# Gathered rows added on TensorE instead of VectorE, in pairs of one kind, with wider compare slots

## The chip, the cores and the metric

One core of one Trainium2 chip. The metric is the device time of one execution in microseconds, the median of three runs.

## The reference

A graph layer over 12,500 nodes with 64 features and 400,000 edges. The edges are sorted by `dst`, and `dst` is drawn so that low nodes have many edges.

```
msg = x[src] + edge_attr
agg = segment_sum(msg, dst, num_segments=12500)
h   = relu(agg @ W1 + b1)
y   = h @ W2 + b2
out = layernorm(x + y)      # over the 64 features, no scale or shift
```

All inputs are float32, `src` and `dst` int32. W1 is 64 x 128, W2 is 128 x 64.

## The kernel before

The sum over edges is done by one-hot products on TensorE, and it has two parts.

**The edge part.** The edges are cut into 625 chunks of 640. A chunk lies in SBUF as 128 partitions x 5 tiles x 64 features. VectorE makes its one-hot (`mark`, L835: node position in a window of 64 nodes, or of 32, against the edge's own), TensorE multiplies the five tiles of rows with the five tiles of the one-hot into `chunk_ps` (`products`, L1059), and VectorE adds the result to `lists`, the sums by node (`add`, L856). Two chunks make a pair: they go to the two halves of the TensorE columns and of the PSUM bank. All of this is float32, and each float32 matmul stands in the trace as two records, so a pair is 10 matmuls and 20 records.

**The x part, in two ways.** The last 205 chunks are *gathered*: GpSimd (POOL) fetches `x[src]` with one indirect DMA for each tile (L572, five a chunk, 1,025 in all) into `xmsg`, and VectorE adds that to the edge rows in `gmsg` (`mix`, L828) before TensorE takes them. The first 420 chunks (`CROWS` = 84 rows of five) are *counted*: nothing is gathered for them. Instead the kernel counts how often each source node occurs for each destination and multiplies these counts by x. A *pass* compares 128 edges of one window of 1 to 4 nodes: VectorE makes two bf16 one-hots for several passes at once (a *slot*, `make_slot`: `oh_lo` L874 and `oh_key` L878, at most 10 passes or 980 key columns), TensorE multiplies them pass by pass into `counted_ps` (L1076), ScalarE copies each finished unit of up to five nodes to `counts` (L674). 128 rows of counts are a *block*; a block is multiplied by x in 98 matmuls of 193 columns (L1092, x split in three bf16 parts), spread by `MULTIPLY` over the slots that follow, and turned (L1104) and added to `lists` (L865). The edges of 128 passes are a *group*: VectorE searches where they begin (L788), POOL fetches their records (L581), TensorE turns them into a table (`turn_table`, L1033).

**What sets the order.** Each engine has one program, written out before the launch. `plan` chooses window width and nodes of each unit by a cost per pass, and fills the slots. `timeline` gives each slot a planned begin, by a cost per slot, between 90 us and `LAST`, and hangs gathers (`GATHERS_AT`) and chunks (`JOBS_AT`) before the slot whose planned begin is due. Nothing waits for a planned time; the engines wait for semaphores only. POOL may gather as far ahead as `xmsg` has buffers (`XSLOTS` = 5 chunks) and waits for `mixed` of the chunk that held the buffer. SP loads the edge rows (`gmsg`, `GSLOTS` = 8, and `cmsg`, `CSLOTS` = 6) as `summed` frees them.

**Before and behind the main loop.** POOL first writes the list of all passes with iotas on one partition (L541, a run of equal windows at a time, once for the node and once for the run). Then it starts to gather; SP sends the list on and loads what the searches need. Behind the loop come the last block, a test whether any count was out of range, and the two-layer network with the norm over node blocks.

## Time and profile before

| | us |
|---|---|
| median of three runs (1505.83 to 1508.44) | 1507.69 |
| the profiled execution | 1504.08 |
| its span, from the first to the last instruction | 1502.3 |
| PE busy, of the span | 1212.9 |
| VectorE (DVE) busy | 1346.7 |
| ScalarE (ACT) busy | 840.6 |
| GpSimd (POOL) busy | 1076.9 |
| mean granted TensorE clock, of 1 | 0.921 |

PE is the matmul side of TensorE and PEld its weight loads, which overlap. Times in the views count from the first instruction of the profiled execution. Instructions of one engine overlap by some tens of ns, so what one costs in a row of many is read from start to start. The slices of the page show three parts: to 86 us preparation, to 1415 us the main loop, and from there the end.

### The profile page before, as it was taken

Reading aid. Unit: us, or ns where it says so; the run is one execution under the profiler, and the core shown is the slowest. Engines: PE = TensorE matmul, PEld = TensorE weight load, DVE = VectorE, ACT = ScalarE, POOL = GpSimd, SP = SyncE. Lnnn points to the kernel's source line nnn. Section 1 sums busy time; section 2 is a strip of 40 time slices with the busy share of each in tenths; the row PEclk is TensorE's granted clock in tenths of the full one; section 3 lists DMA queues with packets and bytes.
Section 4 is the critical chain, followed back from the end, with each engine's and each line's share of the span. In section 5 each row is a group of like instructions: output and inputs, shape, how many; then the busy total and the mean of one; then the engine's idle time right before and its main releaser. Section 6 shows DMA issues by size and latency. Waiting matters only on the chain.

```text
span 1502.3 us, 43214 instructions
## 1 busy us (share of the span) xinstructions
PE 1212.9 (81%) x15541; PEld 979.2 (65%) x15542; DVE 1346.7 (90%) x3537; ACT 840.6 (56%) x1767; POOL 1076.9 (72%) x1139
## 2 busy tenths in 40 slices
PE   1235767778787887888888888899999999999895
PEld 1134656655666776776655555688888888888853
DVE  4659999999999899899999999999999999999644
ACT  1044444668435566567444444567777777766454
POOL 9758777777777777777777777777777777777312
PEclk8555578999999999999999999999999999999997
DMA  2833444444444444444444443444444444433133
GB/s 103 212 85 79 120 113 111 116 111 109 108 115 112 114 115 106 108 109 116 112 114 107 104 117 102 113 112 111 112 112 109 111 113 113 113 100 94 23 79 93
DMA packets 159272, 162.50 MB, mean 108 GB/s; under 512 B 53817, under 2 KB 141801, under 8 KB 158729
## 3 DMA queue, kind: packets, MB, share of 16 engines
q1 hardware_dynamic: 124679, 122.86, 27.9%
q0 software_dynamic: 34384, 36.90, 12.8%
q8 instruction: 126, 2.06, 0.6%
q14 instruction: 83, 0.68, 0.1%
HBM read 154.78 MB, written 4.85 MB: 106 GB/s over the span
## 4 chain that ended last, share of the span: by engine, by line
PE 31%; DVE 29%; issue 16%; POOL 11%; DVEq 4%; ACT 2%; DMA 1%; POOLq 0%; ACTq 0%
PE sums_ps L1092 12%; PE counted_ps L1076 11%; POOL xmsg L572 11%; DVE oh_key L878 10%; DVE oh_lo L874 6%; PE chunk_ps L1059 5%; DVE onehot L835 5%; DVE lists L856 3%; DVE gmsg L828 2%; DVEq L848 2%; PE turn_ps L1104 2%; ACT counts L674 1%; DVE less_b L788 1%; DVEq L856 1%; PE counted_ps L1160 1%
## 5 line engine op out<-in xcount | busy, mean ns | idle before, releaser
L572 POOL DMA_INDIRECT xmsg<-in_x,idx_t x1025 | 995.5, 971 | 322.4 <-issue 307.8
L674 ACT CAST counts<-counted_ps 128x392 bf16<-128x392 f32 (+2 forms) x1375 | 675.2, 545 | 480.6 <-PE counted_ps L1076 468.1
L1076 PE MATMUL counted_ps<-oh_key,oh_lo 128*128 128x196 bf16 (+3 forms) x4206 | 524.7, 255 | 123.2 <-DVE oh_key L878 105.9
L878 DVE TENSOR_TENSOR oh_key<-counted_ps,tables 128x980 bf16<-128x980 f16 (+4 forms) x883 | 541.3, 613 | 0.0
L1092 PE MATMUL sums_ps<-x_parts,counts 128*128 128x193 bf16 (+4 forms) x4410 | 495.0, 249 | 0.3
L1076 PEld LDWEIGHTS counted_ps<-oh_key,oh_lo 128*128 128x128 bf16 x4206 | 290.5, 102 | 227.3 <-DVE oh_key L878 167.0
L1092 PEld LDWEIGHTS sums_ps<-x_parts,counts 128*128 128x128 bf16 (+4 forms) x4410 | 396.3, 109 | 38.6 <-issue 1.9
L874 DVE TENSOR_TENSOR oh_lo<-counted_ps,tables 128x640 bf16<-128x640 f16 (+3 forms) x883 | 412.3, 467 | 9.9 <-PE counted_ps L1076 1.0
L1059 PE MATMUL chunk_ps<-onehot,cmsg 128*64 128x32 f32 (+1 forms) x4200 | 254.1, 231 | 26.2 <-DVE gmsg L828 23.6
L1059 PEld LDWEIGHTS chunk_ps<-onehot,cmsg 128*64 128x64 f32 x4200 | 220.1, 145 | 60.9 <-issue 43.2
L835 DVE TENSOR_TENSOR onehot<-counted_ps,rel_t 128x160 f32<-128x160 f32 (+1 forms) x625 | 234.3, 375 | 0.2
L1059 PE MATMUL chunk_ps<-onehot,gmsg 128*64 128x64 f32 x2050 | 172.8, 238 | 19.8 <-DVE onehot L835 16.7
L1059 PEld LDWEIGHTS chunk_ps<-onehot,gmsg 128*64 128x64 f32 x2050 | 145.1, 148 | 37.4 <-DVE lists L856 26.1
L856 DVE TENSOR_TENSOR lists<-lists,chunk_ps 64x32 f32 (+1 forms) x625 | 121.8, 195 | 43.4 <-PE chunk_ps L1059 17.6
L828 DVE TENSOR_TENSOR gmsg<-gmsg,xmsg 128x320 f32<-128x320 f32 x205 | 97.8, 477 | 2.2 <-DMA xmsg<-in_x,idx_t 2.1
L613 POOL TENSOR_TENSOR x_parts<-x_parts,rstd 128x512 f32<-128x512 f32 (+1 forms) x13 | 12.9, 994 | 76.5 <-DVE rstd L980 76.5
L678 ACT ACTIVATE counted_ps<-counted_ps,less_top 128x392 f32<-128x392 f32 (+2 forms) x100 | 55.5, 555 | 3.2
L581 POOL DMA_INDIRECT records<-edge_records,run_at x33 | 31.7, 959 | 18.0 <-DVE run_at L793 10.3
L1104 PE MATMUL turn_ps<-ident,sums 128*64 128x128 f32 (+4 forms) x270 | 41.9, 295 | 2.6 <-issue 1.9
L1033 PE MATMUL turn_ps<-ident,keys 128*128 128x128 f32 x33 | 11.8, 357 | 38.8 <-DVE keys L803 25.0
L788 DVE TENSOR_SCALAR_CACHE_REDUCE less_b<-most_b,node_t 128x777 bf16<-128x777 int16 (+30 forms) x33 | 30.6, 928 | 13.5 <-DMA most_b<-fine_most 13.1
L650 ACT ACTIVATE tables<-turn_ps,zero 128x512 f16<-128x512 f32 x33 | 22.7, 687 | 35.2 <-PE turn_ps L1034 34.9
(96 smaller groups left out, 450.2 us busy)
## 6 DMA issues: line engine op xcount, KB each, us to landing
cmsg<-in_edge_attr SPq DMA_DIRECT2D x420, 160.0 KB
gmsg<-in_edge_attr SPq DMA_DIRECT2D x205, 160.0 KB
xmsg<-in_x,idx_t POOLq DMA_INDIRECT x1025
x_parts<-in_x SPq DMA_DIRECT2D x12, 256.0 KB, 3.4
out_nodes<-x_parts SPq DMA_DIRECT2D x12, 256.0 KB, 2.6
edge_records<-counts SPq DMA_DIRECT2D x1, 1575.0 KB
lists<-in_src SPq DMA_DIRECT2D x1, 1562.5 KB
lists<-in_dst SPq DMA_DIRECT2D x1, 1562.5 KB
```

Source lines behind the costliest of these rows:

```text
L572: pool.indirect_dma_start(xmsg[:, at * D:(at + 1) * D], None, x, bass.IndirectOffsetOnAxis(ap=idx_t[:, of:of + 1], axis=0)).then_inc(gathe ...
L674: nc.scalar.copy(to, ps.rearrange("p (n h) -> p h n", h=HI)).then_inc(unit_kept, 1)
L678: nc.scalar.activation(ps, ps, ACT.Relu, bias=less_top[:, 0:1], accum_out=over[:, k:k + 1]).then_inc(unit_checked, 1)
L828: nc.vector.tensor_tensor(to, to, xmsg[:, t * TILES * D:(t + 1) * TILES * D], ALU.add).then_inc(mixed, 1)
L835: nc.vector.tensor_tensor(onehot[place % OSLOTS][:, 0:TILES * w].rearrange("p (j n) -> p j n", j=TILES), node_ps[:, 0:w].unsqueeze(1).broa ...
L856: nc.vector.tensor_tensor(to, to, chunk_ps[place // 2 % 2][place % 2 * D:(place % 2 + 1) * D, 0:w], ALU.add).then_inc(added, 1)
L874: nc.vector.tensor_tensor(oh_lo[s % RING][:, 0:n * P].rearrange("p (k n o) -> p k n o", k=n, o=2), lo_ps.rearrange("p (n o) -> p n o", o=2 ...
L878: nc.vector.tensor_tensor(oh_key[s % RING][:, 0:n * w].rearrange("p (k n o) -> p k n o", k=n, o=2), key_ps[:, 0:w].rearrange("p (n o) -> p ...
L1059: mm = nc.tensor.matmul(chunk_ps[place // 2 % 2][half * D:(half + 1) * D, 0:w], rows[half][:, j * D:(j + 1) * D], onehot[place % OSLOTS][: ...
L1076: mm = nc.tensor.matmul(unit_ps[u % BANKS][:, col:col + slot.key_cols], oh_lo[s % RING][:, n * P:(n + 1) * P], oh_key[s % RING][:, n * slo ...
L1092: mm = nc.tensor.matmul(sums_ps[0:n, 0:XC], counts[b % 2][:, h * P:h * P + n], x_parts[:, h * XC:(h + 1) * XC], start=(h == 0), stop=(h == ...
L1104: mm = nc.tensor.matmul(turn_ps[0:D, 256:256 + n], sums[0:n, k * D:(k + 1) * D], ident[0:n, 0:n], start=(k == 0), stop=(k == PARTS - 1))
```

## The change

TensorE takes the gathered rows as they come: a gathered chunk's product is over ten tiles (five of `gmsg`, five of `xmsg`) with the one-hot used twice, and `mix` is gone. Pairs are of one kind, gathered with gathered and counted with counted; one VectorE instruction makes the one-hots of both chunks, so `onehot` has two buffers of double width. POOL waits for `summed` in place of `mixed`; `XSLOTS` is 6 and `GSLOTS` 6. Slots take up to 12 passes or 12 window nodes. `plan` and `timeline` have other costs. 86 rows of chunks are counted, so 430 chunks, and 195 are gathered. `subtract` moves one slot earlier on VectorE and `turn_table` one later on TensorE. Loads and stores over 125, 84 or 86 rows are cut at a multiple of 16 rows.

Of the tables only the sums are told: 4,206 passes in 883 slots, 33 groups and 45 blocks before; 5,104 passes in 598 slots, 40 groups and 48 blocks now. Window nodes over all passes: 8,096 before, 6,940 now. `LAST` is 1435.2 before and 1349.75 now.

```diff
-CROWS = 84
+CROWS = 86
+SLOT = 12
@@ plan
-            cost = sum(t * (195 + 92 * w) for t in ts) / nodes
+            cost = sum(t * (85 + 86 * w) for t in ts) / nodes
-        while (at + n < len(passes) and (at + n) % P and passes[at + n][2] == width and n < 10
-               and (n + 1) * width * hi <= 10 * hi):
+        while (at + n < len(passes) and (at + n) % P and passes[at + n][2] == width and n < SLOT
+               and (n + 1) * width <= SLOT):
@@ timeline
-    cost = [x.n * (195 + 92 * x.width) + 500 for x in slots]
+    cost = [x.n * (67 + 51 * x.width) + 290 for x in slots]
-    FIRST, LAST = 90.0, 36.0 + 6.6 * gathered + 1.4 * groups
+    FIRST, LAST = 90.0, 36.0 + 6.45 * gathered + 1.4 * groups
+    pairs = [(36.0 + chunk * (k + 2) + 5.0, "gather", k) for k in range(0, gathered - 1, 2)]
+    pairs += [(70.0 + (LAST - 70.0) * (i + 1.) / counted, "count", i) for i in range(0, counted - 1, 2)]
+    pairs.sort()
...
+        jobs_at[s] += [(2 * q, kind, i), (2 * q + 1, kind, i + 1)]
@@ build
-    SUBTRACT = at_slots([(max(0, GROUP_FIRST[g] - 5), g) for g in later])
-    TURN_TABLE = at_slots([(max(0, GROUP_FIRST[g] - 6), g) for g in later])
+    SUBTRACT = at_slots([(max(0, GROUP_FIRST[g] - 6), g) for g in later])
+    TURN_TABLE = at_slots([(max(0, GROUP_FIRST[g] - 5), g) for g in later])
-    OSLOTS = 4
+    OSLOTS = 2
-    GSLOTS, XSLOTS, CSLOTS = 8, 5, 6
+    GSLOTS, XSLOTS, CSLOTS = 6, 6, 6
@@ sync
-            sp.dma_start(src_i, src_v).then_inc(src_in, 16)
-            sp.dma_start(dst_i, dst_v).then_inc(dst_in, 16)
+            for to, of, done in ((src_i, src_v, src_in), (dst_i, dst_v, dst_in)):
+                for a, b in in_sixteens(ROWS):
+                    sp.dma_start(to[a:b, :], of[a:b, :]).then_inc(done, 16)
@@ gpsimd, gather
-                    pool.wait_ge(mixed, k - XSLOTS + 1)
+                    pool.wait_ge(summed, PLACE["gather", k - XSLOTS] + 1)
@@ vector
-            def mix(k):
...
-                nc.vector.tensor_tensor(to, to, xmsg[:, t * TILES * D:(t + 1) * TILES * D], ALU.add).then_inc(mixed, 1)
+            def mark(pair):
+                (place, kind, i), n = pair[0], len(pair) * TILES
+                c, w = i if kind == "count" else CCH + i, width_of(kind, i)
+                if place >= 2 * OSLOTS:
+                    dve.wait_ge(summed, place - 2 * OSLOTS + 2)
                 nc.vector.tensor_tensor(
+                    onehot[place // 2 % OSLOTS][:, 0:n * w].rearrange("p (j n) -> p j n", j=n),
+                    node_ps[:, 0:w].unsqueeze(1).broadcast_to([P, n, w]),
+                    rel_t[:, c * TILES:c * TILES + n].unsqueeze(2).broadcast_to([P, n, w]),
@@ tensor
-                s = i % GSLOTS
-                pe.wait_ge(mixed, i + 1)
-                return gmsg[:, s * TILES * D:(s + 1) * TILES * D]
+                s, t = i % GSLOTS, i % XSLOTS
+                pe.wait_ge(gin[s], 16 * (i // GSLOTS + 1))
+                pe.wait_ge(gathered[t], 16 * TILES * (i // XSLOTS + 1))
+                return [gmsg[:, s * TILES * D:(s + 1) * TILES * D], xmsg[:, t * TILES * D:(t + 1) * TILES * D]]
@@ tensor, products
+                steps = [[(of, j) for of in parts for j in range(TILES)] for parts in rows]
+                for n in range(max(len(x) for x in steps)):
                     for half, (place, kind, i) in enumerate(pair):
...
+                mm.then_inc(summed, len(pair))
```

Three places show how the built programs differ.

TensorE late in the main loop, before the change: passes, block products and pairs of chunks take turns.

```order
L1076 MATMUL counted_ps<-oh_key,oh_lo 128x196 x5
L1092 MATMUL sums_ps<-x_parts,counts 128x193 x10
L1059 MATMUL chunk_ps<-onehot,cmsg 64x32 x10
L1076 MATMUL counted_ps<-oh_key,oh_lo 128x196 x5
L1092 MATMUL sums_ps<-x_parts,counts 128x193 x10
L1076 MATMUL counted_ps<-oh_key,oh_lo 128x196 x5
L1092 MATMUL sums_ps<-x_parts,counts 128x193 x9
L1059 MATMUL chunk_ps<-onehot,gmsg 64x64
L1059 MATMUL chunk_ps<-onehot,cmsg 64x32
```

The same after it (the line numbers are those of the changed kernel; L1065 is `products`, L1081 the passes, L1097 the block products):

```order
L1081 MATMUL counted_ps<-oh_key,oh_lo 128x196 x6
L1097 MATMUL sums_ps<-x_parts,counts 128x193 x12
L1065 MATMUL chunk_ps<-onehot,gmsg 64x64 x10
L1065 MATMUL chunk_ps<-onehot,xmsg 64x64 x10
L1065 MATMUL chunk_ps<-onehot,cmsg 64x32 x10
L1081 MATMUL counted_ps<-oh_key,oh_lo 128x196 x6
L1097 MATMUL sums_ps<-x_parts,counts 128x193 x12
```

A pair with a gathered chunk was 10 matmuls, five of each chunk in turn; a pair of two gathered chunks is 20, and there are 97 such pairs and one single chunk.

VectorE late in the main loop, before (an `ISA` row sets a register):

```order
L874 TENSOR_TENSOR oh_lo0<-counted_ps,tables0 128x640
L878 TENSOR_TENSOR oh_key0<-counted_ps,tables0 128x980
L835 TENSOR_TENSOR onehot2<-counted_ps,rel_t 128x320
L828 TENSOR_TENSOR gmsg<-gmsg,xmsg 128x320
L856 ISA
L856 TENSOR_TENSOR lists<-lists,chunk_ps0 64x64
L835 TENSOR_TENSOR onehot3<-counted_ps,rel_t 128x320
```

And after:

```order
L838 TENSOR_TENSOR onehot1<-counted_ps,rel_t 128x640
L859 ISA
L859 TENSOR_TENSOR lists<-lists,chunk_ps0 64x64
L877 TENSOR_TENSOR oh_lo2<-counted_ps,tables1 128x768
L881 TENSOR_TENSOR oh_key2<-counted_ps,tables1 128x1176
```

The mix is gone, one instruction makes two one-hots, and a slot is of 6 passes where it was of 5.

POOL before its first gather; before the change these iotas were 48 instructions with 8,448 elements, among them two of 1,426, two of 1,064 and two of 542. After it:

```order
L551 IOTA counts 1x80 x2
L551 IOTA counts 1x210 x2
L551 IOTA counts 1x668 x2
L551 IOTA counts 1x272 x2
L551 IOTA counts 1x2145 x2
L551 IOTA counts 1x1564 x2
```

They are 30 instructions with 10,240 elements; the last run of 1,564 is the passes of the late part of the loop, with windows of two nodes and one run of 128 edges a window (1,426 before).

## Rows read from the trace of the kernel before

**Rows 1.** The page's first part: busy time of each engine, share of the span, instructions.

```profile
PE 1212.9 (81%) x15541; PEld 979.2 (65%) x15542; DVE 1346.7 (90%) x3537; ACT 840.6 (56%) x1767; POOL 1076.9 (72%) x1139
```

**Rows 2.** Busy time by stretch, with granted clock (of 1), DMA share and GB/s.

```profile
86.00:975.00 889.00, 705.25 (x9319) 551.73 (x9320) 843.99 (x2305) 477.06 (x952) 672.87 (x693) 0.91 0.42 110
...
975.00:1400.00 425.00, 411.49 (x5579) 360.68 (x5580) 411.70 (x1087) 298.48 (x730) 319.72 (x334) 1.00 0.41 108
```

**Rows 3.** The timeline of POOL: start, us, instruction, idle time before it.

```profile
39.71 4.42 POOL L572 DMA_INDIRECT xmsg<-in_x,idx_t  x1 [0.16 <-issue]
...
75.72 0.94 POOL L572 DMA_INDIRECT xmsg<-in_x,idx_t  x1 [0.31 <-issue]
...
87.01 0.95 POOL L572 DMA_INDIRECT xmsg<-in_x,idx_t  x1 [10.35 <-DVE gmsg L828]
...
110.88 3.32 POOL L572 DMA_INDIRECT xmsg<-in_x,idx_t  x1 [0.30 <-issue]
...
1406.16 0.94 POOL L572 DMA_INDIRECT xmsg<-in_x,idx_t  x1 [0.30 <-issue]
```

**Rows 4.** POOL's groups from 86 to 1408 us: busy us, mean ns, idle before.

```profile
L572 POOL DMA_INDIRECT xmsg<-in_x,idx_t x1000 | 968.4, 968 | 314.9 <-issue 300.3 <-DVE gmsg L828 14.6
L581 POOL DMA_INDIRECT records<-edge_records,run_at x31 | 29.8, 960 | 17.3 <-DVE run_at L793 10.3 <-issue 7.0
```

**Rows 5.** The timeline of PE at 1104 us.

```profile
1104.03 0.78 PE L1059 MATMUL chunk_ps<-onehot,cmsg 128*64 128x32 f32 x20
1104.74 0.60 PE L1076 MATMUL counted_ps<-oh_key,oh_lo 128*128 128x196 bf16 x5
1105.17 1.02 PE L1092 MATMUL sums_ps<-x_parts,counts 128*128 128x193 bf16 x10
1106.03 0.59 PE L1076 MATMUL counted_ps<-oh_key,oh_lo 128*128 128x196 bf16 x5
```

**Rows 6.** PE's groups from 975 to 1400 us, by shape.

```profile
L1092 PE MATMUL sums_ps<-x_parts,counts 128*128 128x193 bf16 x2071 | 211.2, 247 | 0.3
...
L1076 PE MATMUL counted_ps<-oh_key,oh_lo 128*128 128x196 bf16 x1356 | 168.8, 248 | 12.2 <-ACT counts L674 6.6 <-DVE oh_key L878 4.0
...
L1059 PEld LDWEIGHTS chunk_ps<-onehot,cmsg 128*64 128x64 f32 x1350 | 66.0, 137 | 10.7 <-issue 10.2 <-DVE lists L865 0.2 <-DVE lists L856 0.2
...
L1059 PEld LDWEIGHTS chunk_ps<-onehot,gmsg 128*64 128x64 f32 x650 | 42.7, 137 | 5.2 <-issue 4.4 <-DVE lists L856 0.3
...
L1104 PE MATMUL turn_ps<-ident,sums 128*64 128x128 f32 x132 | 18.9, 280 | 0.0
```

**Rows 7.** The timeline of PE where the main loop ends.

```profile
1414.71 8.60 PE L1092 MATMUL sums_ps<-x_parts,counts 128*112 128x193 bf16 x98
```

**Rows 8.** POOL's first 37 us by shape: busy us, mean ns.

```profile
L541 POOL IOTA counts<- 1x1426 int16 x2 | 12.1, 6052 | 0.0
...
L541 POOL IOTA counts<- 1x1064 int16 x2 | 9.1, 4552 | 0.0
```

**Rows 9.** The timeline of DVE where the main loop begins.

```profile
85.86 0.49 DVE L835 TENSOR_TENSOR onehot<-counted_ps,rel_t 128x320 f32<-128x320 f32 x1
```

**Rows 10.** The timeline of PE, the first pair of chunks.

```profile
87.69 1.33 PE L1059 MATMUL chunk_ps<-onehot,gmsg 128*64 128x64 f32 x20 [1.29 <-DVE gmsg L828]
```

**Rows 11.** The timeline of PE at 1344 us, two chunks with windows of 64.

```profile
1344.33 0.22 PE L1059 MATMUL chunk_ps<-onehot,cmsg 128*64 128x64 f32 x1
1344.34 0.22 PE L1059 MATMUL chunk_ps<-onehot,gmsg 128*64 128x64 f32 x1
1344.39 0.22 PE L1059 MATMUL chunk_ps<-onehot,cmsg 128*64 128x64 f32 x1
```

**Rows 12.** DVE's groups of the whole run, by shape.

```profile
L874 DVE TENSOR_TENSOR oh_lo<-counted_ps,tables 128x640 bf16<-128x640 f16 x391 | 188.8, 483 | 4.1
...
L874 DVE TENSOR_TENSOR oh_lo<-counted_ps,tables 128x1280 bf16<-128x1280 f16 x145 | 118.7, 819 | 2.2
...
L828 DVE TENSOR_TENSOR gmsg<-gmsg,xmsg 128x320 f32<-128x320 f32 x205 | 97.8, 477 | 2.2 <-DMA xmsg<-in_x,idx_t 2.1
```

More of the change, by code:

```diff
@@ L106, in narrow_chunks, with in_sixteens @@
     return count
+def in_sixteens(rows):
+    return (0, rows // 16 * 16), (rows // 16 * 16, rows)
 def within(value, top):
@@ L128, in timeline @@
         gathers_at[s].append(divmod(g, 5))
-    jobs = [(36.0 + chunk * (k + 1) + 5.0, "gather", k) for k in range(gathered)]
-    jobs += [(70.0 + (LAST - 70.0) * (i + .5) / counted, "count", i) for i in range(counted)]
-    jobs.sort()
+    pairs = [(36.0 + chunk * (k + 2) + 5.0, "gather", k) for k in range(0, gathered - 1, 2)]
+    pairs += [(70.0 + (LAST - 70.0) * (i + 1.) / counted, "count", i) for i in range(0, counted - 1, 2)]
+    pairs.sort()
     jobs_at = [[] for _ in range(S + 1)]
     s = 0
-    for place, (_, kind, i) in enumerate(jobs):
-        t = jobs[min(place | 1, len(jobs) - 1)][0]
+    for q, (t, kind, i) in enumerate(pairs):
         while s < S and begin[s] < t:
             s += 1
-        jobs_at[s].append((place, kind, i))
+        jobs_at[s] += [(2 * q, kind, i), (2 * q + 1, kind, i + 1)]
+    kind, i = ("gather", gathered - 1) if gathered % 2 else ("count", counted - 1)
+    jobs_at[S].append((2 * len(pairs), kind, i))
     return gathers_at, jobs_at
@@ L164, in build @@
     NARROW_ROWS = narrow_chunks(N, E, CHUNK, SLIM, CCH) // TILES
-    width_of = lambda kind, i: SLIM if kind == "count" and i < NARROW_ROWS * TILES else WIN
+    width_of = lambda kind, i: SLIM if kind == "count" and (i | 1) < NARROW_ROWS * TILES else WIN
     HI = -(-N // P)
@@ L309, in build @@
         list_i = [onehot[1][0:GROUPS, k * P // 2:(k + 1) * P // 2].bitcast(i16) for k in range(2)]
-        list_f = [onehot[2][0:GROUPS, k * P:(k + 1) * P] for k in range(2)]
+        list_f = [onehot[1][0:GROUPS, (k + 1) * P:(k + 2) * P] for k in range(2)]
         XH = HI // 2
@@ L364, in build @@
         gathered = [sem(f"gathered{s}") for s in range(XSLOTS)]
-        mixed = sem("mixed")
         marked, summed, added = sem("marked"), sem("summed"), sem("added")
@@ L889, in _ @@
             for s in range(NS + 1):
-                for place, kind, i in JOBS_AT[s]:
-                    mark(place, kind, i)
-                    if kind == "gather":
-                        mix(i)
-                    if place >= LAG:
-                        add(place - LAG)
+                for k in range(0, len(JOBS_AT[s]), 2):
+                    pair = JOBS_AT[s][k:k + 2]
+                    mark(pair)
+                    for place, _, _ in pair:
+                        if place >= LAG:
+                            add(place - LAG)
                 if s == NS:
```

57 lines of the change are left out of this document (23 added, 34 removed).

## The prediction

> **What bounds the kernel now.** I read the busy shares first: VectorE 90%, PE 81%, POOL 72% [rows 1]. The page counts POOL's issue time as idle, so its share misleads. In the timeline of POOL a gather takes 0.94 to 0.95 us, and 0.30 or 0.31 us of issue lie ahead of each: one every 1.25 us [rows 3]. POOL's first gather starts at 39.71 us, the last at 1406.16 [rows 3]. From 87.01 on it issues 1,000 gathers and 31 record fetches [rows 4]; 1,031 x 1.25 = 1288.8 us of the 1320.1 until 1407.1. So POOL is bound through the whole loop. The other 31.4 us: gathers longer than 0.946 us, 968.4 - 946.0 = 22.4; waits for VectorE's searches, 10.3 less eight ordinary issues of 0.3 = 7.9; 1 is not explained [rows 4]. Of the 22.4, four gathers of 3.0 to 3.4 us, of which the row at 110.88 shows one, make 9.0: they lie beside VectorE's subtractions of 3,136 columns. The other 13.4 I put down to the mixes.
>
> The windows show who is near POOL. From 86 to 975 us VectorE is busy 844.0 of 889 (95%) and PE 705.3 (79%). From 975 to 1400 both are full: VectorE 411.7 of 425, PE 411.5 (97%), at a granted clock of 1.00 [rows 2]. The late part is that of the blocks with 64 passes each. PE's own time there, from start to start in its timeline: five passes 0.43 us (86 ns each), ten block matmuls 0.86 (86 ns), a pair of chunks with 20 records 0.71 [rows 5]. The groups have 2,071 block matmuls and 1,356 passes, 2,000 chunk records or 100 pairs, and 18.9 us of turned sums [rows 6]: 3,427 x 0.086 + 100 x 0.71 + 18.9 = 384.6 us. The remaining 40.4 (9.5%) are short waits, table turns and changes of kind.
>
> **The change, part by part.**
>
> *POOL, fewer issues.* 975 gathers and 40 record fetches against 1,025 and 33.
>
> *POOL, the start.* The iotas ahead of the first gather cost 4.1 ns an element between the two largest (6.052 - 4.552 us over 362) [rows 8]. By that slope 2,145 elements take 9.0 us and 1,564 take 6.6; with the small runs I get 42.6 us where the 48 before took 34.7. So gathers start 8 us later, at 48; SP's loads for the searches wait for the same list, and VectorE's loop, which begins at 85.86 [rows 9], begins at 93 (8 less 0.9 for two edge loads that go behind). The cut loads over 112 + 13 rows bring `dst` earlier, but the list is then last: nothing gained. Six buffers let POOL do 30 gathers and two fetches (48.2 + 3.5 + 32 x 1.25 = 91.7 us) before it waits. It waited 10.35 us, until 87.01, with 25 gathers done [rows 3]. Now the first pair needs its one-hots (0.73 us) and a product of 40 records at the low clock. 20 records took 1.33 us there [rows 10]; so 2.4. POOL goes on at 96.5.
>
> *POOL, to the end.* 96.5 + 983 x 1.25 = 1325.3. I keep 9.0 for the four subtractions and 7.9 for the searches, and drop the mixes' 13.4 (it could stay: 0 to 13). POOL ends at 1343, 64 us earlier. If nothing else bound, the kernel would take 1504.1 - 64 = 1440 us in the profiled execution.
>
> *VectorE.* The mixes were 97.8 us. A one-hot instruction has a fixed part: 640 columns 483 ns, 1,280 columns 819 [rows 12], so 0.525 ns a column and 147 ns fixed. Columns in the slots hardly change: 5,104 x 128 + 6,940 x 98 = 1.333 million against 1.332. Slots fall from 883 to 598 with two instructions each: 570 x 0.147 = 84 us. 312 chunk one-hots fewer: 46. Seven searches more with their tables cost 12. VectorE falls from 1347 to 1131 us busy, 78% of the new span. It no longer binds, so of these 216 us only the freer gathers above are worth anything.
>
> *TensorE, the gathered chunks.* Each has 20 records instead of 10. What a record of a pair gathered with gathered costs is not in the trace at the high clock. The nearest is a pair in which both windows are 64: three records, alternating halves, at 1344.33, .34 and .39, so two each 0.06 us [rows 11], as with windows of 32. So 20 more records cost 0.58 us and such a pair 0.71 + 0.58 = 1.29. The Trainium skill, "TensorE: Matmul & The Clock Gate", section "Measured speedup vs the span model", says that a weight load overlaps matmuls in flight only when the row group differs; here all products use all rows, so by it each record would pay load and stream. The trace speaks against it for two column halves [rows 11], and I keep it as a rival below.
>
> *TensorE, the passes.* The last 1,564 passes are 24.4 blocks of 64, with 24.4 x 98 = 2,395 block matmuls. By the plan's cost they take 261 slots x 1,304 of 869,000, or 39% of the 1,260 us between 90 and `LAST`: 493 us by plan, with 73 gathered and 166 counted chunks. POOL does 365 gathers and 12 fetches in 471 us, 475 with its stretch. PE needs 3,959 x 0.086 = 340.5, 83 counted pairs x 0.71 = 58.9, 36.5 gathered pairs x 1.29 = 47.1, and 21 for the turned sums: 467.5 us. With the remainder of before (9.5% of the time) it is 516.6. Part of that remainder was PE waiting for ScalarE and VectorE [rows 6], and would go as PE falls behind; changes of kind and table turns stay. I take two thirds: 500 us. Earlier in the loop PE's load is some 42 us per 50 by plan and POOL's 48, so PE follows the gathers there. `turn_table` behind `subtract` takes waits from PE in that part only, and POOL hides it.
>
> **The sum.** POOL has done the gathers ahead of the late part (all but 365) at 96.5 + 606 x 1.25 + 14 = 868 us. PE then needs 500: 1368. Before, the same place, where 98 block matmuls stand alone behind the loop, was at 1414.7 [rows 7]. That is 46.7 us less; what follows is unchanged. 1504.1 - 46.7 = 1457.4 in the profiled execution. The median stands 3.6 us above that execution: **1461 us**, 3.1% faster.
>
> **The rivals.**
>
> *PE binds late (the forecast), 0.50.* Between the remainder gone (then POOL binds) and kept whole (516.6, end at 1385): medians 1447 to 1478.
>
> *POOL binds to the end, 0.28.* PE's remainder is waiting and vanishes. For it: PE has 467.5 against 475. Then 1440 + 3.6 = 1444, and down to 1437 if the waits for searches go too, as VectorE is free. Against it: 97% busy at 92% of that load.
>
> *Gathered pairs cost double, 0.09.* If each record pays load and stream, the pair costs 1.1 us more. 36.5 such pairs add 40 us late, and the middle, at 42 + 4 of 48, just holds: about 1500. [rows 11] speak against it.
>
> *Lockstep, slower, 0.06.* A gathered pair now waits on TensorE for its second chunk's landing, and the passes behind it, VectorE's adds and then its next one-hots wait too. POOL stalls only when six chunks are full. If each of the 97 waits costs more than VectorE's slack, (1250 - 1040)/97 or about 2 us in the loop (1,040 being its 1,131 less the part outside the loop), plus half a us for the 47 us gained, the kernel is slower than before; at 3 us it is 1560. Against: before, TensorE waited for `mixed` in the same way and POOL lost only 14.6 us in 15 waits [rows 4].
>
> *The rest, 0.07:* a lower granted clock late, where PE has no slack. Each 50 us at half clock would cost 25 us; but in this part it was 1.00 [rows 2].
>
> **How the numbers follow.** Best guess 1461. The first two cases reach from 1437 to 1478 and hold 0.78; the range is **1437 to 1482**, with a little of the third and fifth. About 0.2% (3 us) is what a measurement of this kernel can tell from no change. Nearly all cases lie below 1505: faster 0.92, same 0.02, slower 0.06.
>
> **What would show it.** POOL's first gather near 48 us, its first long wait ending near 96. Gathers at 1.25 us, with the stretched ones gone but for four. PE over 98% busy in the last 500 us of the loop, and POOL waiting there for `chunk_ps` once it is six chunks ahead, or PE's last block matmuls well behind the last gather: more than 15 us means PE, under 10 means POOL. VectorE busy near 1131. A gathered pair 1.3 us from start to start; 2 or more would prove me wrong. VectorE and PE both idle ahead of gathered pairs all through the middle would be the lockstep.

## The result

The changed kernel takes 1542.49 us (median of three runs, 1537.16 to 1544.24) where the kernel before takes 1507.69. The ratio is 1.0225, 95% interval 1.0183 to 1.0267: a little over 2% slower, clear of no change. The forecast was 1461 us, 3.1% faster, with 1437 to 1482 as its range.

One thing is needed to read the runs further down: in all but the last two, the kernels took some 1.7 times as long (the kernel before 2549 to 2551 us instead of 1508, the changed one 2615 instead of 1542, mean granted clock 0.71 to 0.81), for a reason that the traces do not show, so there only ratios to the kernel before, measured beside each, are compared; the changed kernel had 1.0251 among them (1.0229 to 1.0272).

### The profile page after: what moved, and what is told of

Same layout as the page of the kernel before. It is cut to its first block, busy times and chain, and to the rows that moved or that the text cites. A ratio compares the mean times of both kernels' runs of the same rounds, so it can differ in the third digit from the quotient of the medians.

```text
span 1540.7 us, 47757 instructions
## 1 busy us (share of the span) xinstructions
PE 1231.5 (80%) x18715; PEld 1081.2 (70%) x18716; DVE 1228.7 (80%) x2488; ACT 813.9 (53%) x1619; POOL 1024.1 (66%) x1078
## 4 chain that ended last, share of the span: by engine, by line
PE 54%; DVE 19%; issue 9%; DVEq 6%; ACT 4%; POOL 1%; DMA 0%; POOLq 0%; ACTq 0%
PE sums_ps L1097 22%; PE counted_ps L1081 16%; PE chunk_ps L1065 12%; DVE oh_key L881 8%; DVE oh_lo L877 5%; DVEq L851 4%; ACT counts L684 3%; DVE lists L859 2%; PE turn_ps L1109 1%; DVE onehot L838 1%; DVE less_b L798 1%; DVEq L859 1%; PE counted_ps L1165 1%; ACT lists L654 1%; POOL x_parts L623 1%
## 5 line engine op out<-in xcount | busy, mean ns | idle before, releaser
L684 ACT CAST counts<-counted_ps 128x392 bf16<-128x392 f32 (+1 forms) x1368 | 688.3, 581 | 538.8 <-PE counted_ps L1081 529.7
L1081 PE MATMUL counted_ps<-oh_key,oh_lo 128*128 128x98 bf16 (+1 forms) x5104 | 446.9, 231 | 202.9 <-DVE oh_key L881 175.1
L1081 PEld LDWEIGHTS counted_ps<-oh_key,oh_lo 128*128 128x128 bf16 x5104 | 321.8, 102 | 281.1 <-DVE oh_key L881 217.8
L1097 PE MATMUL sums_ps<-x_parts,counts 128*128 128x193 bf16 (+3 forms) x4704 | 483.3, 252 | 0.0
L881 DVE TENSOR_TENSOR oh_key<-counted_ps,tables 128x1176 bf16<-128x1176 f16 (+2 forms) x598 | 441.4, 738 | 0.0
L877 DVE TENSOR_TENSOR oh_lo<-counted_ps,tables 128x768 bf16<-128x768 f16 (+3 forms) x598 | 430.8, 720 | 10.9 <-PE counted_ps L1081 3.1
L1097 PEld LDWEIGHTS sums_ps<-x_parts,counts 128*128 128x128 bf16 (+3 forms) x4704 | 420.4, 118 | 2.1 <-issue 0.2
L859 DVE TENSOR_TENSOR lists<-lists,chunk_ps 64x32 f32 (+1 forms) x625 | 122.4, 196 | 196.2 <-PE chunk_ps L1065 147.7
L838 DVE TENSOR_TENSOR onehot<-counted_ps,rel_t 128x320 f32<-128x320 f32 (+1 forms) x313 | 191.1, 611 | 1.5
L1065 PE MATMUL chunk_ps<-onehot,cmsg 128*64 128x32 f32 (+1 forms) x4300 | 174.4, 230 | 0.6 <-issue 0.6
L1065 PEld LDWEIGHTS chunk_ps<-onehot,cmsg 128*64 128x64 f32 x4300 | 151.2, 144 | 26.8 <-issue 13.3
L591 POOL DMA_INDIRECT records<-edge_records,run_at x40 | 37.8, 944 | 109.9 <-DVE run_at L803 106.2
L1065 PE MATMUL chunk_ps<-onehot,gmsg 128*64 128x64 f32 x1950 | 81.9, 233 | 3.1 <-DVE lists L859 2.0
L1065 PEld LDWEIGHTS chunk_ps<-onehot,gmsg 128*64 128x64 f32 x1950 | 69.2, 144 | 14.1 <-issue 6.7
L1065 PE MATMUL chunk_ps<-onehot,xmsg 128*64 128x64 f32 x1950 | 77.9, 228 | 0.0
L1065 PEld LDWEIGHTS chunk_ps<-onehot,xmsg 128*64 128x64 f32 x1950 | 69.7, 144 | 0.0
L1109 PE MATMUL turn_ps<-ident,sums 128*64 128x128 f32 (+3 forms) x288 | 41.6, 282 | 1.3 <-DVE lists L868 0.9
L551 POOL IOTA counts<- 1x14 int16 (+12 forms) x30 | 41.6, 1423 | 0.0
```

Source lines behind the costliest of these rows:

```text
L684: nc.scalar.copy(to, ps.rearrange("p (n h) -> p h n", h=HI)).then_inc(unit_kept, 1)
L838: nc.vector.tensor_tensor(onehot[place // 2 % OSLOTS][:, 0:n * w].rearrange("p (j n) -> p j n", j=n), node_ps[:, 0:w].unsqueeze(1).broadca ...
L859: nc.vector.tensor_tensor(to, to, chunk_ps[place // 2 % 2][place % 2 * D:(place % 2 + 1) * D, 0:w], ALU.add).then_inc(added, 1)
L877: nc.vector.tensor_tensor(oh_lo[s % RING][:, 0:n * P].rearrange("p (k n o) -> p k n o", k=n, o=2), lo_ps.rearrange("p (n o) -> p n o", o=2 ...
L881: nc.vector.tensor_tensor(oh_key[s % RING][:, 0:n * w].rearrange("p (k n o) -> p k n o", k=n, o=2), key_ps[:, 0:w].rearrange("p (n o) -> p ...
L1065: mm = nc.tensor.matmul(chunk_ps[place // 2 % 2][half * D:(half + 1) * D, 0:w], of[:, j * D:(j + 1) * D], onehot[place // 2 % OSLOTS][:, ( ...
```

## The profile after

The page's first part of the changed kernel, to be laid beside [rows 1]:

```profile
span 1540.7 us, 47757 instructions
PE 1231.5 (80%) x18715; PEld 1081.2 (70%) x18716; DVE 1228.7 (80%) x2488; ACT 813.9 (53%) x1619; POOL 1024.1 (66%) x1078
```

VectorE lost 118 us of work and POOL 53; TensorE gained only 19. The span grew by 38. So the time went into waits. The chain that ended last, by engine (before: PE 31%, DVE 29%, issue 16%, POOL 11%):

```profile
PE 54%; DVE 19%; issue 9%; DVEq 6%; ACT 4%; POOL 1%; DMA 0%; POOLq 0%; ACTq 0%
```

POOL is off the chain, as forecast. But TensorE was not full either. The waits of the whole run, who waited for whom, us in total, times, longest:

```profile
PE counted_ps L1081 <- DVE oh_key L881: 175.1, 170, 7.5
DVE lists L859 <- PE chunk_ps L1065: 147.7, 92, 8.9
POOL records L591 <- DVE run_at L803: 106.2, 28, 9.5
POOL xmsg L582 <- PE chunk_ps L1065: 17.2, 27, 9.3
```

The first three before the change, in the same order: 105.9, 17.6 and 10.3 us. TensorE has no wait for a DMA of edge or gathered rows in that list, so the smaller `gmsg` (6 buffers for 8) did not hold it. The reader should see a circle: TensorE waits for VectorE's key one-hots, VectorE waits in `add` for TensorE's products, and POOL waits for VectorE's searches, which stand behind its adds in its written order. The windows (us, busy time of each engine, clock, DMA share, GB/s) show what that leaves of the late part; compare [rows 2]:

```profile
93.00:925.00 832.00, 663.98 (x11204) 595.66 (x11206) 721.68 (x1436) 433.15 (x753) 603.84 (x630) 0.92 0.42 111
925.00:1440.00 515.00, 477.26 (x6942) 424.65 (x6939) 419.58 (x930) 324.23 (x802) 333.19 (x354) 0.99 0.38 100
```

TensorE is busy 92.7% and VectorE 81% of the late part, where both had 97%. From 896 us to the loop's end TensorE's waits for key one-hots are 29.0 us, where [rows 6] had 4.0 in 425. One turn of the circle, in VectorE's timeline (start, us, instruction, idle time before it and what ended it) of the changed kernel:

```profile
663.89 0.48 DVE L838 TENSOR_TENSOR onehot<-counted_ps,rel_t 128x320 f32<-128x320 f32 x1
664.29 0.40 DVE L859 TENSOR_TENSOR lists<-lists,chunk_ps 64x32 f32 x2
664.72 0.82 DVE L838 TENSOR_TENSOR onehot<-counted_ps,rel_t 128x640 f32<-128x640 f32 x1
668.70 0.48 DVE L859 TENSOR_TENSOR lists<-lists,chunk_ps 64x32 f32 x2 [3.16 <-PE chunk_ps L1065]
...
669.41 0.94 DVE L877 TENSOR_TENSOR oh_lo<-counted_ps,tables 128x1536 bf16<-128x1536 f16 x1
670.28 0.75 DVE L881 TENSOR_TENSOR oh_key<-counted_ps,tables 128x1176 bf16<-128x1176 f16 x1
```

and TensorE's timeline of the same microseconds:

```profile
665.93 0.70 PE L1081 MATMUL counted_ps<-oh_key,oh_lo 128*128 128x98 bf16 x12
666.47 1.37 PE L1097 MATMUL sums_ps<-x_parts,counts 128*125 128x193 bf16 x14
667.77 0.78 PE L1065 MATMUL chunk_ps<-onehot,cmsg 128*64 128x32 f32 x20
...
671.09 0.71 PE L1081 MATMUL counted_ps<-oh_key,oh_lo 128*128 128x98 bf16 x12 [1.35 <-DVE oh_key L881]
```

Two pairs fall in one slot here, a counted one and a gathered one. VectorE makes the counted pair's one-hots at 663.89 and the gathered pair's at 664.72, and behind these its program asks for the counted pair's product. TensorE works in the same order, and has a slot's 12 passes and a share of block matmuls to do before it: the product starts at 667.77, the add at 668.70. For 3.16 us VectorE makes nothing; its store of ready slots runs out, and TensorE waits 1.35 us at 671.09 for the next key one-hots.

I sorted these waits by where the pairs stand in the written order: each add belongs to a pair, and is asked for where the next pair is marked. "Distance" is the number of slots between the two. Worked out from the timeline's L859 rows (L856 before) and the tables; five waits of 6.9 us that belong to no such pair, four of them ahead of the second add of a pair and one behind the last pair, are left out (five of 5.4 us before):

```
slots to the next pair:                 0       1       2      3      4 and more
before:  pairs                          5       19      119    89     80
         us waited for the product      3.5     5.7     3.1    0      0
after:   pairs                          47      64      88     95     18
         us waited for the product      100.3   35.7    4.9    0      0
```

136 of 141 us lie where the next pair is in the same slot or the next one (8.9 of them in one wait at the end of the loop). The change has 111 such places instead of 24, because gathered and counted pairs are now spaced by two rules that know nothing of each other; before, all chunks stood in one row by time and two neighbours made a pair. A slot is not the same stretch of time in the two: there are 598 now for 883.

The loop ends, at the row that answers to [rows 7], 34.6 us later, with the block before it done in one lump too:

```profile
1434.96 8.55 PE L1097 MATMUL sums_ps<-x_parts,counts 128*128 128x193 bf16 x98
...
1449.28 8.55 PE L1097 MATMUL sums_ps<-x_parts,counts 128*36 128x193 bf16 x98
```


## The experiments

Theory A: lockstep of VectorE and TensorE through the adds. Theory B: the searches hold POOL. Theory C: TensorE's own work is the bound. Ratios are to the kernel before, measured beside each. In the traces of all but d5 and d6 many waits end with no releaser that the trace knows (`remote`).

| kernel | us | ratio | interval |
|---|---|---|---|
| e1_lag4 | 2508.28 | 0.9847 | 0.9825 to 0.9869 |
| e2_apart | 2583.4 | 1.0133 | 1.0109 to 1.0157 |
| e3_search | 2531.24 | 0.994 | 0.9917 to 0.9964 |
| e4_both | 2465.9 | 0.968 | 0.9658 to 0.9702 |
| a0_after | 2614.97 | 1.0251 | 1.0229 to 1.0272 |
| a1_lag4 | 2514.48 | 0.9864 | 0.9842 to 0.9886 |
| a2_both | 2470.82 | 0.9688 | 0.9669 to 0.9707 |
| a3_oldplan | 2613.42 | 1.0249 | 1.0224 to 1.0275 |
| b1_before_lag4 | 2527.11 | 0.9906 | 0.9879 to 0.9934 |
| b2_before_pesum | 2447.37 | 0.9602 | 0.9573 to 0.963 |
| b3_after_mix | 2668.16 | 1.0458 | 1.0426 to 1.0489 |
| b4_before_both | 2435.2 | 0.954 | 0.9512 to 0.9567 |
| d1_rows86 | 2480.23 | 0.9731 | 0.9704 to 0.9758 |
| d2_onekind | 2663.62 | 1.0445 | 1.042 to 1.0469 |
| d3_rows84 | 2626.85 | 1.0296 | 1.027 to 1.0321 |
| d4_best | 2286.43 | 0.897 | 0.8945 to 0.8996 |
| d5_spread | 1502.68 | 0.9989 | 0.998 to 0.9997 |
| d6_onekind_lag4 | 1496.09 | 0.994 | 0.9926 to 0.9954 |

**Later adds (e1_lag4).** The changed kernel with each add four places behind its one-hots.

```diff
-    LAG = 2
+    LAG = 4
```

> The changed kernel with LAG = 4 in place of 2: VectorE adds a pair's product to the sums one pair later, behind the one-hots of the pair after next. Nothing else moves. Theory A (lockstep on VectorE's adds: in the changed kernel VectorE waits 147.7 us in 92 waits for the product of the pair just marked, most where two pairs stand before one slot, and TensorE then waits for the slots behind them): these waits fall below 40 us, TensorE's waits for oh_key fall from 175 us below 100, and the time falls by 40 to 70 us from 1542, below the kernel before (1508). Theory B (POOL is held by the searches, 106 us in 28 waits, and the rest follows it): the time stays within 10 us of 1542. Theory C (TensorE's own work is the bound): it falls by at most 15 us.

It takes 3.9% off the changed kernel (0.9847, and 0.9864 against 1.0251 when repeated as a1_lag4). The changed kernel at this pace (a0_after) had VectorE waiting 449.1 us in `add` for products and 488.8 more there with no known releaser, and TensorE 134.2 for key one-hots; here it is 10.2, none and 34.8. But VectorE's waiting moved more than it went: it now waits 348.2 us for passes ahead of `oh_lo` (93.6 in a0_after) and 74.1 for products ahead of its one-hots, with 413.9 and 225.1 more of no known releaser. The time has A's sign; by C it would have moved by 1% at most.

**Pairs apart (e2_apart).** The changed kernel with no two pairs before one slot, though still in neighbouring ones.

```diff
-        while s < S and begin[s] < t:
+        while s < S and (begin[s] < t or (t > 90.0 and s == last)):
             s += 1
+        last = s
```

> The changed kernel with its pairs of chunks placed so that no two stand before the same slot in the main loop: a pair that would share a slot with the one ahead of it goes to the next (47 pairs share a slot in the changed kernel, 5 before the change and 5 here, all at the start). LAG stays 2. Theory A: most of the gain of the longer lag is seen here too, 25 to 55 us less than 1542, with VectorE's waits for products below 80 us. Theory B and C: within 10 us of 1542.

1.2% off, and the forecast of A for the waits (below 80 us) fails: VectorE still waits 422.7 us for products. The pairs that shared a slot are now one slot apart, and that is too near as well: 290 of these us lie at the 117 places where the next pair is in the next slot.

**Earlier searches (e3_search), and both (e4_both).** The loads and searches of a group four slots earlier, the fetches where they were; then this with `LAG` = 4.

```diff
-    SEARCH_LOAD = at_slots([(max(0, GROUP_FIRST[g] - 18), g) for g in later])
-    SEARCH = at_slots([(max(0, GROUP_FIRST[g] - 11), g) for g in later])
+    SEARCH_LOAD = at_slots([(max(0, GROUP_FIRST[g] - 22), g) for g in later])
+    SEARCH = at_slots([(max(0, GROUP_FIRST[g] - 15), g) for g in later])
...
-                for g in SEARCH.get(s - 3, []):
+                for g in SEARCH.get(s - 7, []):
```

> The changed kernel with the searches on VectorE four slots earlier (15 ahead of a group's first slot, not 11) and their loads too; POOL's record fetches stay in their place, 8 slots ahead. Theory B: POOL's waits for run_at fall from 106 us below 30, gathers come earlier, and the time falls by 30 to 60 us. Theory A: POOL's waits for run_at fall as well, but POOL only waits for its buffers instead (waits for chunk_ps of 50 us or more), and the time stays within 8 us of 1542.

> Both edits: LAG = 4 and the searches four slots earlier. If A alone holds, the time is that of the longer lag alone within 5 us. If, once the lockstep is gone, POOL is what is late, the earlier searches give a further 5 to 20 us. My sum for a loop paced by POOL or TensorE was 1444 to 1478; theory C expects 1525 or more.

Searches alone: 3.0% off. Both: 5.6% off, so the two gains add only in part (3.9 and 3.0). B holds beside A, as far as these long runs go; POOL's wait for searches there is 784.8 us in a0_after, 442.3 with the earlier searches and 316.6 with both.

**The changed kernel again, and its plan (a0_after, a3_oldplan).** The second has slots of 10 and the costs and `LAST` of before.

```diff
-SLOT = 12
+SLOT = 10
-            cost = sum(t * (85 + 86 * w) for t in ts) / nodes
+            cost = sum(t * (195 + 92 * w) for t in ts) / nodes
-    cost = [x.n * (67 + 51 * x.width) + 290 for x in slots]
+    cost = [x.n * (195 + 92 * x.width) + 500 for x in slots]
```

> The changed kernel as it stands, timed once more beside the others of this call and beside the kernel before. All theories: 1.0225 of the kernel before, as in the first comparison (1.018 to 1.027), TensorE's pace and VectorE's as there (VectorE waiting for the chunks' products 148 us, TensorE waiting for key one-hots 175 us). It anchors the ratios of the other three.

> The changed kernel with the numbers of before for the plan: slots of at most 10 passes, the costs 195 + 92 w and 195 + 92 w with 500, and 6.6 us a gathered chunk. TensorE's sums of gathered rows, the pairs of one kind and the 86 counted rows stay. Theory A in the form that wide slots do it (a slot of 12 passes holds two pairs where one of 10 held one, so that the adds of the second wait for the first's slot): the waits of VectorE for products fall from 148 us to under 60 and the time falls by 1.5 to 3%, 1495 to 1520. A in the form that the gathered pair's longer product does it: within 0.7% of the changed kernel, 1530 to 1553. B: POOL's wait for searches falls where slots are smaller, since the searches then lie closer ahead only in passes; 1530 to 1545. C: more instructions for VectorE and as many for TensorE: 1540 to 1555.

No difference: 1.0249 against 1.0251. The wide slots are not the cause, and the VectorE instructions that they save are worth nothing here. VectorE waits 257.9 us in `add` for products where a0_after has 449.1, at the same time of the kernel; its waits for passes ahead of `oh_lo` are larger instead (199.6 for 93.6). So the size of this one wait does not give the time at this pace.

**The two repeats (a1_lag4, a2_both).**

> The changed kernel with the adds of the chunks' products four places behind their one-hots instead of two, so that VectorE asks for a pair's product one pair later. Theory A (VectorE in lockstep with TensorE through the adds): the 148 us that VectorE waits for the chunks' products fall under 20, TensorE's 175 us for key one-hots fall with them, and the time falls by 2 to 4%: 1480 to 1510 us where the kernel before takes 1508. Theory B (POOL held by the searches): within 0.5% of the changed kernel, 1535 to 1545. Theory C (TensorE's own work binds late, as forecast, only dearer): 1530 or more, since PE was at 93% there.

> The changed kernel with the adds four places behind and the searches of the groups four slots earlier. If A and B both hold and add up, it is below the one with the later adds alone by a part of the 106 us that POOL waits for the searches in the changed kernel: 1455 to 1490 us where the kernel before takes 1508. If A alone holds, it is within 0.3% of the one with the later adds alone. C: 1530 or more.

Both give what e1_lag4 and e4_both gave, within 0.2%.

**The same edits before the change (b1_before_lag4, b4_before_both).**

> The kernel before with the adds four places behind their one-hots instead of two, nothing else. Theory A1 (the lockstep through the adds is new in the changed kernel: before, VectorE waited for the gathered rows in its own mixes and so never ran ahead to an add whose product was still to come): within 1% of the kernel before, 0.99 to 1.00. Theory A2 (both kernels lose as much by it, and the change only adds to it): 0.96 to 0.98, as the same edit does to the changed kernel (0.962 of it). Theory C (TensorE's own work): 1.00.

> The kernel before with both edits that made the changed kernel faster: adds four places behind, and the searches, their loads four slots earlier with the record fetches where they were. It tells what the change is worth when these two waits are out of the way in both: the changed kernel with them has 0.969 of the kernel before. Theory A1: the kernel before gains little, 0.98 to 1.00, so the change is then worth 1 to 3%. Theory A2: 0.95 to 0.97, so the change is worth nothing or costs even then. Theory B (searches alone) 0.985 to 0.995.

Later adds are worth 0.9% there, against 3.9% in the changed kernel: what later adds cure is mostly new. Both edits give 0.954, where A1 had 0.98 to 1.00. The earlier searches on top of the later adds are thus worth 3.7% in the kernel before (0.9906 to 0.954), no less than in the changed one: at this pace POOL's wait for searches is no mark of the change. And the changed kernel with both edits has 0.969, so with the same two edits on either side the change still costs 1.6%: the adds are not all of it.

**TensorE's sums alone (b2_before_pesum) and taken out (b3_after_mix).** The first has of the change only this:

```diff
-                    if kind == "gather":
-                        mix(i)
...
-                pe.wait_ge(mixed, i + 1)
-                return gmsg[:, s * TILES * D:(s + 1) * TILES * D]
+                pe.wait_ge(gin[s], 16 * (i // GSLOTS + 1))
+                pe.wait_ge(gathered[t], 16 * TILES * (i // XSLOTS + 1))
+                return [gmsg[:, s * TILES * D:(s + 1) * TILES * D], xmsg[:, t * TILES * D:(t + 1) * TILES * D]]
```

The second is the changed kernel with the mixes put back.

> The kernel before with one part of the change alone: TensorE takes a gathered chunk's edge rows and its gathered node rows as two operands, and VectorE's mixes are gone; pairs of both kinds, a one-hot for each chunk, slots of 10 and 84 counted rows stay. Theory A1 (who waits for the gathers is what matters: now TensorE waits, with VectorE's add behind it): slower than the kernel before by 1 to 3%, ratio 1.01 to 1.03, with VectorE's wait for the products up from 18 us to over 100. Theory D (the pairs of one kind and their single one-hot instruction do it, the adds of a pair being asked for together): 0.97 to 1.00. Theory C (TensorE's extra products bind): 1.01 to 1.02 with VectorE's wait for products under 50.

> The changed kernel with VectorE adding the gathered rows again (a mix for each gathered chunk behind the pair's one-hots, TensorE waiting for it, and POOL too), the rest of the change kept. Theory A1: VectorE is paced by the gathers again, its wait for products falls under 50 us; 205 mixes of 0.5 us come back; ratio to the kernel before 0.98 to 1.005, that is faster than the changed kernel by 2% or more. Theory D: as slow as the changed kernel or slower, 1.02 to 1.04. Theory C: 1.00 to 1.01, TensorE having 1,950 records less.

My theory A1 of that moment (TensorE, not VectorE, now waits for the gathers, and the adds behind it stand) falls: the sums alone are 4% *faster* (outside the ranges of all three theories), and the mixes put back make the changed kernel 2% slower. The part of the change on which the forecast spent most of its sum is the good part.

**Rows, pairs of one kind, and the best (d1 to d4).** d1_rows86 is b2_before_pesum with `CROWS = 86`; d3_rows84 is the changed kernel with `CROWS = 84`; d2_onekind is b2_before_pesum with the pairs of the changed kernel, each chunk with its own one-hot:

```diff
-    jobs = [(36.0 + chunk * (k + 1) + 5.0, "gather", k) for k in range(gathered)]
-    jobs += [(70.0 + (LAST - 70.0) * (i + .5) / counted, "count", i) for i in range(counted)]
-    jobs.sort()
+    pairs = [(36.0 + chunk * (k + 2) + 5.0, "gather", k) for k in range(0, gathered - 1, 2)]
+    pairs += [(70.0 + (LAST - 70.0) * (i + 1.) / counted, "count", i) for i in range(0, counted - 1, 2)]
+    pairs.sort()
```

with `subtract` and `turn_table` in the changed kernel's order and six buffers of each kind. d4_best is b2_before_pesum with later adds and earlier searches.

> The kernel before with TensorE adding the gathered rows (ratio 0.960 to the kernel before) and 86 counted rows instead of 84: ten gathered chunks fewer, ten counted ones more, 7 groups and searches more, 64 passes a block for longer; slots of 10 and pairs of both kinds stay. Theory R (the two more counted rows cost what the change loses: 38 searches instead of 31 hold POOL, and 7% more passes load TensorE): 0.98 to 1.02. Theory P (the pairs of one kind do it): 0.955 to 0.97. Theory H (the one-hots of a pair in one instruction do it): the same as P.

> The kernel before with TensorE adding the gathered rows and pairs of one kind by the changed kernel's rule for their slots (with its order of subtraction and table turn, and six buffers for each of edge and gathered rows, which such pairs need), but a one-hot instruction of its own for each chunk, 84 rows, slots of 10. Theory P: most of what the change loses appears, 0.99 to 1.03. Theory R and theory H: 0.955 to 0.97.

> The changed kernel with 84 counted rows instead of 86, everything else kept (slots of 12, the new costs, pairs of one kind with one one-hot instruction). Theory R: 0.96 to 0.985 of the kernel before. Theories P and H: 1.01 to 1.025.

> The kernel before with TensorE adding the gathered rows, the adds four places behind and the searches four slots earlier; nothing else of the change. If the three gains add up (0.960, 0.954): 0.91 to 0.93. If they remove the same waits: 0.94 to 0.955.

The pairs of one kind cost 8.8% (0.960 to 1.0445, above the range that P gave), with the buffers and the order of `subtract` and `turn_table` that came with them and were not tried alone; 86 rows cost 1.3% on the faster kernel, between the two ranges that were forecast, and nothing in the changed one (1.0296 with 84, 1.0251 with 86). d4_best is 10.3% faster than the kernel before, better than both of its ranges (0.91 to 0.93, 0.94 to 0.955) and than the single gains together (0.960 x 0.954 = 0.916).

**Where the pairs fall (d5_spread), or the pair itself (d6_onekind_lag4).** Both start from d2_onekind.

```diff
+    free = 0.0
     for q, (t, kind, i) in enumerate(pairs):
+        t = max(t, free)
+        free = t + 3.7
```

> The last kernel with pairs of one kind (ratio 1.0445), with its pairs spread: each pair is placed at least 3.7 us by plan behind the one before it, so that 5 pairs instead of 34 share a slot with the pair before them and 18 instead of 53 follow in the next slot, as in the kernel before (5 and 18). Theory P1 (pairs of one kind fall together, since gathered and counted pairs are spaced apart from each other by two rules, and each such meeting has VectorE's adds wait for TensorE): 0.96 to 0.98. Theory P2 (the pair itself does it: two gathered chunks needed at once, 40 records in a lump, POOL's six buffers let go two at a time): 1.02 to 1.045.

> The same kernel with pairs of one kind, not spread, with the adds four places behind. Theory P1: the meetings no longer make an add wait: 0.96 to 0.99, at least 0.05 below 1.0445. Theory P2: the adds were not what was waited for: 1.01 to 1.03, no more than the 1% to 3% that the same edit gave elsewhere.

These two ran at the pace of the first comparison (the kernel before 1503.87 us beside them), and d2_onekind was not run there. So P1 is not proved by d5 against d2; what they show is that a kernel with TensorE's sums and pairs of one kind is no slower than before at this pace when the pairs stand apart (0.9989) or the adds come later (0.994). Both are above what P1 gave (0.96 to 0.98 and 0.96 to 0.99). The waits of the two, d5 first:

```profile
PE counted_ps L1080 <- DVE oh_key L882: 121.2, 159, 6.9
DVE lists L860 <- PE chunk_ps L1064: 55.5, 53, 3.1
POOL records L585 <- DVE run_at L797: 26.2, 9, 5.8
```

```profile
PE counted_ps L1077 <- DVE oh_key L879: 94.9, 101, 7.0
POOL records L582 <- DVE run_at L794: 19.2, 8, 3.2
DVE lists L857 <- PE chunk_ps L1061: 4.6, 6, 1.3
```

Against 175.1, 147.7 and 106.2 in the changed kernel all three are down, and the search wait falls though no search was moved. That fits a consequence of VectorE's delay, but the two also have 33 groups for 40 and slots of 10. In d5, 24 pairs stand in the same or the next slot (111 in the changed kernel); they have 20.4 of its 52.3 us. Another 29.5 us lie two slots apart, where the kernel before, with nearly the same distances, had 3.1: distance is not all, and a VectorE without mixes comes to its adds sooner. POOL is on the chain again (33% in d5 and 31% in d6, beside 36% and 39% of TensorE; 1% in the changed kernel), and in d6 the late part is full, as [rows 2] had it:

```profile
900.00:1407.00 507.00, 493.11 (x7149) 432.85 (x7147) 457.50 (x1221) 338.27 (x820) 362.36 (x384) 1.00 0.41 104
```

There the freed VectorE is worth about what its mixes had stretched in POOL's gathers. POOL's groups of d6 from 86 us on, beside [rows 4]:

```profile
L573 POOL DMA_INDIRECT xmsg<-in_x,idx_t x995 | 948.8, 954 | 310.0 <-issue 297.2 <-PE chunk_ps L1061 12.5 <-PE turn_ps L1033 0.3
```

954 ns instead of 968 over 1,000 gathers is 14 us; POOL's last gather starts at 1394.96 instead of 1406.16 [rows 3].

## Why the prediction was wrong

**Right, each near its number.** POOL's first gather at 46.66 us (48), its first long wait ending at 95.83 (96.5). The iotas 41.6 us (42.6). A gathered pair from start to start 1.19 us (1.29) where turned sums follow, and 1.32 where passes do (the median of 13 between 975 and 1400 us):

```profile
1100.10 0.80 PE L1065 MATMUL chunk_ps<-onehot,gmsg 128*64 128x64 f32 x20
1100.70 0.78 PE L1065 MATMUL chunk_ps<-onehot,xmsg 128*64 128x64 f32 x20
1101.29 0.82 PE L1109 MATMUL turn_ps<-ident,sums 128*64 128x128 f32 x6
```

So the rival of double cost, 2.4 us, is out, and with it the rule as the prediction took it from the Trainium skill ("TensorE: Matmul & The Clock Gate"; the sentence stands there in the section "The mechanism"). The gathers' stretch went with the mixes (954 ns a gather). TensorE, not POOL, ended the loop: its last block matmuls begin 20 us behind POOL's last gather (1428.90), where more than 15 was to mean PE. The granted clock was 0.99 late.

**The step that failed:** "It no longer binds" of VectorE, and with it "PE then needs 500: 1368". I summed each engine's own work and let the largest be the bound, with VectorE at 78% out of the account. Its busy time was only mis-sized (1228.7 us, 80%, against 1131): the terms for slots, one-hots and mixes came out near (81, 43 and 98 us for 84, 46 and 98), but they are durations of instructions that overlap one another, and with 1,049 fewer of them the overlap itself fell from 222 to 135 us. The error is that an engine below full still binds when its program asks for something that another has yet to reach. 147.7 us of waits in `add` were not in the sum, though the new order, in which pairs meet, could be counted from the tables. They do not add to the time one for one: the loop missed its forecast by 81 us.

**Where the 81 us between 1368 and 1449 lie.** The late part was to begin at 868 us, with 610 gathers issued; POOL had issued 610 at 896: 28 us. In POOL's own rows ahead of 896 they are mostly its waits for VectorE's searches, 38.5 us in 16, where the sum had 7.9 for the whole loop. It then lasted 553 us instead of 500, the other 53:

```profile
896.00:1449.28 553.28, 512.02 (x7444) 455.06 (x7442) 443.85 (x989) 344.89 (x850) 355.18 (x377) 0.99 0.38 99
```

My 467.5 us were counted from start to start; by the busy column the same count gave 384.6 where [rows 2] show 411.5, a factor 1.07, so 500 was TensorE busy without a pause. It was busy 512: the work was right within 2.4%. The 41 us of idle time are the miss. The other 4 us of the 85 by which the profiled execution missed 1457.4 lie behind the loop.

**"I keep [...] 7.9 for the searches"** was wrong by 90 us (106.2 in 28 waits, 97.8 without the ordinary issue). It does not add to the above: what of it lies ahead of 896 us is the 28 already counted, and behind 896, where 67.4 us of it lie, POOL still ended 20 us ahead of TensorE. d5 and d6, with 26.2 and 19.2, suggest that it follows VectorE's delay.

**"`turn_table` behind `subtract` takes waits from PE":** the wait of TensorE for the keys, 25.0 us before, is gone from the list, and that bought nothing that can be seen.

**The lockstep rival** had the sign and got 0.06. Its mechanism was half right. The adds wait for TensorE and then the one-hots wait for the adds, as it said. But it looked for the cause in a gathered pair's landing rows, whereas counted pairs wait as well (62.5 of the 141 us), and most of the waiting goes by the distance to the next pair. It set its threshold by VectorE's spare time, 2.5 us on each of 97 pairs; 92 waits of 1.6 us sufficed, since TensorE had no spare time to lose. The argument against it, that TensorE waited for `mixed` in the same way before, was no evidence: that wait stopped TensorE, not VectorE. b3_after_mix, slower still with the old kind of wait, speaks against the kind of wait as the cause. Its sum for 3 us a pair was also off: (3 - 2.16) x 97 is 81 us over 1461, so 1542 and not 1560. That this is the measured time is luck, since the waits had another size, number and place.

**What is shown, what is not.** Shown at the first pace: the waits, their places, that the late part's work was right, and that a close relative with spaced pairs or later adds has smaller waits than the changed kernel and times of 0.999 and 0.994. No single edit of the changed kernel was measured at that pace, so the cause of its 2% is read from its trace there and not proved by taking it away. Shown at the slower pace alone: that later adds in the changed kernel itself take 3.9% off, that pairs of one kind with their buffers cost 8.8%, rows 1.3%, the plan nothing, and that TensorE's sums alone gain 4%. How large these are at 1508 us is open. So is why the changed kernel with both edits stays behind the kernel before with both (0.969 and 0.954), and whether d4_best's 10% would be more than the 0.6% of d6 where POOL's gathers, 1.25 us each, bind.

## What to carry to other kernels

When two engines pass work to and fro in written orders, count in those orders how far behind its request each product lies: a request for something that the other has not reached stops both, whatever their busy shares are. A change of grouping can bring many of these distances to nothing and leave every sum of work as it was; look at the histogram before the sums. And test an engine's "spare" time against the places where it must answer within a slot, not against the whole loop.

## What the runs showed of the hardware

TensorE takes a 64 x 64 float32 record on alternating halves of its columns about every 30 ns. Late in the loop of the changed kernel, 20 records up to the passes behind them took 0.71 us with 32 columns of one-hot and 0.73 with 64; a gathered pair's 40 took 1.32, so the added ten tiles cost 0.6 us a pair and no more.

VectorE's full-width float32 additions had stretched POOL's gathers. In the kernel before, the 220 gathers that lie beside a mix took 1,008 ns in the mean and the 776 others 946, the four long ones aside: 13.75 us in all, the 13.4 that the prediction put down to the mixes. Without mixes the mean is 954 instead of 968 ns, long ones included, at the same issue distance of 0.30 us.

In the long runs VectorE's and POOL's instructions took as long as ever. The key one-hots of the changed kernel (L881) took 738 ns in the mean in the first comparison and 737 there. What grew was idle time, much of it with no releaser. TensorE's timeline of a0_after, the longest such pause:

```profile
995.74 0.78 PE L1065 MATMUL chunk_ps<-onehot,cmsg 128*64 128x32 f32 x20
...
999.41 0.25 PE L1081 MATMUL counted_ps<-oh_key,oh_lo 128*128 128x98 bf16 x2 [1.13 <-issue]
1019.94 0.57 PE L1081 MATMUL counted_ps<-oh_key,oh_lo 128*128 128x98 bf16 x5 [20.28 <-issue]
```

POOL went on gathering every 1.25 us through it. VectorE asked for the product at 995.74, by these rows done at 996.5, after its one-hots of 1000.41, and got it only here:

```profile
1005.95 0.47 DVE L859 TENSOR_TENSOR lists<-lists,chunk_ps 64x32 f32 x2 [5.06 <-remote]
```

So in the long runs TensorE's rows do not tell when its products are there for others, and the waits read from these traces are rough. What held TensorE there isn't in the trace.
